# Cross-attention in fp32 from paired fp32r products: the division of the softmax moved from VectorE to ScalarE

## The chip, the cores and the metric

The kernel runs on one core of a Trainium2 chip. The metric is the device time of one execution in microseconds (us). The core has engines with a queue of instructions each: the matrix engine TensorE (PE), VectorE (DVE), ScalarE (ACT), GpSimd (POOL) and SyncE (SP), which here only starts transfers. Each engine takes its own instructions in order; between engines order is kept by semaphores.

## The reference

Input are `x` and `ctx`, each 8 batches of 256 tokens by 512. A first layer mixes them without a softmax. Then the data pass two cross-attention layers of 16 heads of width 128 and an MLP of width 2048, each behind a layer norm and added to its input. Cut to the attention:

```
h = layer_norm(x)
qh, kh, vh = heads(h @ wq + bq), heads(ctx @ wk + bk), heads(ctx @ wv + bv)
kh, vh = concat(kh, bias_k), concat(vh, bias_v)        # one more key and value: 257
logits = einsum('bqhk,bthk->bhqt', qh, kh) / sqrt(128)
weights = softmax(logits, axis=-1)
x = x + einsum('bhqt,bthk->bqhk', weights, vh).reshape(b, q, 2048) @ wo + bo
```

All is float32.

## The kernel before

Every large product is made from three matmuls in the fp32r type (`product`, lines 487 to 491): both operands are held as a high part and a low part, and hi*hi, lo*hi and hi*lo are summed in PSUM. So each result that is to be an operand again is split: ScalarE writes the high part (`qT_hi`, `kT_hi`, `v_hi`, `PT_hi`, `oT_hi`), and VectorE then the rest (`qT_lo` and so on). The weights are split by GpSimd, a cast (line 398) and a subtraction (line 400) of 128x1024 for each matrix.

The batches are done in two halves of four. A half is the first layer, two attention layers and the MLP. An attention layer is eight bodies, one for each pair of heads: FIRST, six MIDDLE in a loop, and LAST (FINAL in the second layer). A body has units of projection (q, k, v and the output product w, 2048 columns wide in two halves or one) in a ring of four PSUM banks `U`, and eight items. An item is one head of one batch: its logits go to `S` (step L), the softmax gives `probs`, PE transposes them to `T` (step T), ScalarE and VectorE split them into `PT_hi` and `PT_lo`, and PE multiplies them with the values into `O` (step P). The order is written out by hand in `ORDER` (lines 105 to 114) as one string for each kind of body, and every engine walks the same string:

```
MIDDLE: "uuuu L0 uuu L1 T0 uu P0 u L2 T1 uu P1 u L3 T2 uu P2 u L4 T3 uu P3 u "
        "L5 T4 uu P4 u L6 T5 uu P5 L7 T6 uu P6 u T7 uu P7 uuu",
```

`u` is half a unit. PE does these steps as written. VectorE takes the row maximum at L (line 1018), and at T the low part of the turned item (line 1032) and then `divide` of the item after it (lines 1020 to 1028). ScalarE at T turns the high part (line 813) and then does `softmax` of the item after (lines 800 to 808): two exponentials of 128x257, each with its sum in `sums`. `divide` waits for them, takes the reciprocal `rs`, waits for that, and multiplies `probs` in place in two instructions of 128x256, after which `a_prob` lets PE transpose. `probs`, `nm`, `sums` and `rs` have two slots each, `S`, `T` and `O` one. In between, ScalarE and VectorE do the splits of the units at their `u` (lines 785 to 798 and 985 to 1008), among them the two small copies that put the extra key into `kT` (line 943).

Of the kernel before, what the change touches and what calls it, by code (L numbers as in the profile page):

```python
# [30 lines left out]
ALU = mybir.AluOpType  # L31
ACT = mybir.ActivationFunctionType
# [35 lines left out]
def units_of(kind):  # L68

    return [u for u in UNITS_A if kind != FINAL or u[0] not in "KV"]  # L70
# [7 lines left out]
def before(half, e, what):  # L78

    return half * ((HBODIES - 1) * per_body(what) + per_body(what, FINAL)) + e * per_body(what)  # L80


def nth(units, c, what):

    return sum(u[0] in what for u in units[:c + 1])
# [31 lines left out]
def steps(kind):  # L117

    halves = [(c, s) for c, u in enumerate(units_of(kind)) for s in ((1,) if u[0] == "w" else (0, 1))]
    normed = int(kind == FIRST)  # L120
    out = []
    for word in ORDER[kind].split():
        if word[0] == "u":
            for _ in word:
                out.append(("U", *halves.pop(0)))
        elif word == "Z":
            out.append(("Z", normed))
        elif word[0] == "A":
            out.append(("A", normed, int(word[1:])))
        else:  # L130
            out.append((word[0], int(word[1:])))
    assert not halves
    return out


def norm_units(kind):

    after = steps(kind)
    after = after[[a[0] for a in after].index("Z"):]
    begun = [a[1] for a in after if a[0] == "U" and (a[2] == 0 or units_of(kind)[a[1]][0] == "w")]  # L140
    assert len({c % RING for c in begun[:CH]}) == CH
    return begun[:CH]


def item(j):

    return j // 4, (j % 4) // 2, j % 2
# [30 lines left out]
def bass_xattn(nc, x_in, ctx_in, thw, thb, pgw, pgb, www, bncol, wa, wk, wv, wb, hcol, vrow,  # L178
               lncol, f1col, orow, out):
    ctx = ExitStack()  # L180
    with ctx:
        def sb(name, shape, dt=F32):
            return ctx.enter_context(nc.sbuf_tensor(name, [P, *shape], dt))
# [5 lines left out]
        def sem(name):  # L189
            return ctx.enter_context(nc.semaphore(name))  # L190
# [32 lines left out]
        probs = sb("probs", [2, 2, 258])  # L223
# [18 lines left out]
        rs = sb("rs", [2, 2])  # L242
# [41 lines left out]
        a_max, a_exp, a_rcp, a_prob = (sem("a_" + s) for s in ("max", "exp", "rcp", "prob"))  # L284
# [6 lines left out]
        def bank(c):  # L291
            return U[:, c % RING, :]

        def qslot(part, h):
            return qT[part][:, h, :]

        def kview(part, p, h):
            return kT[part][:, p, h, :, 0:256]

        def vview(part, p, pair_of):  # L300
            return v[part][:, p, 2 * pair_of:2 * pair_of + 2, :]

        def two(ap):
            return ap.rearrange("p (a n) -> p a n", a=2)

        def kept(eng, value):

            return value if isinstance(value, int) else eng.snap(value)

        def wait_apart(eng, sem, value):  # L310


            eng.wait_ge(sem, value)
            eng.sem_inc(apart, 1)
# [413 lines left out]
        def _(act):  # L728
# [37 lines left out]
            def norm(l, li, p, ch, c):  # L766

                k = CH * p + ch
                wait_apart(act, ln_T, l * TURNS + k + 1)
                wait_apart(act, ln_h, l * TURNS + k - 1 + CR2)  # L770
                act.activation(aff[:, k % 2, :], bank(c), ACT.Identity, bias=lnc[:, 1, li * CH + ch:li * CH + ch + 1],
                               scale=lnc[:, 0, li * CH + ch:li * CH + ch + 1]).then_inc(ln_affine, 1)
                act.wait_ge(ln_affine, l * TURNS + k + 1)
                act.activation(hT[0][:, ch, p * 512:p * 512 + 512], aff[:, k % 2, :], ACT.Copy).then_inc(ln_hi, 1)

            def attention(half, layer, g, kind):
                e = layer * BODIES + g
                n = half * HBODIES + e
                units = units_of(kind)
                ub = act.snap(before(half, e, ALL))  # L780
                jb = act.snap(n * ITEMS)
                vu = act.snap(before(half, e, VS))
                head = kept(act, e * 2)

                def unit_hi(c):

                    what, p, i = units[c]
                    if what == "q":
                        wait_apart(act, a_unit, ub + c + 1 + CR1)
                        act.activation(qslot(0, i), bank(c), ACT.Identity,  # L790
                                       bias=hc[:, 0, bass.ds(head + i, 1)]).then_inc(a_hi, 1)
                    elif what in "kK":
                        wait_apart(act, a_unit, ub + c + 1 + CR1)
                        act.activation(kview(0, p, i), two(bank(c)), ACT.Identity,
                                       bias=hc[:, 1, bass.ds(head + i + 2 * (what == "K"), 1)]).then_inc(a_hi, 1)
                    elif what in "vV":
                        act.wait_ge(a_v32, vu + nth(units, c, VS))
                        act.activation(vview(0, p, i), two(tmp[:, i, :]), ACT.Copy).then_inc(a_hi, 1)  # L798

                def softmax(j):  # L800

                    act.wait_ge(a_max, jb + j + 1)
                    act.wait_ge(a_T, jb + j - 1 + CR2)
                    for qt in range(2):
                        ins = act.activation(probs[:, j % 2, qt, 0:257], S[:, qt, 0:257], ACT.Exp,  # L805
                                             bias=nm[:, j % 2, qt:qt + 1], scale=-1.0,
                                             accum_out=sums[:, j % 2, qt:qt + 1])
                    ins.then_inc(a_exp, 1)

                def turned_hi(j):  # L810
                    act.wait_ge(a_T, jb + j + 1 + CR2)
                    act.wait_ge(a_pv, jb + j + CR1)
                    act.activation(PT[0][:], T[:], ACT.Copy).then_inc(a_pthi, 1)  # L813

                def o_hi(j):
                    p, h, b = item(j)
                    wait_apart(act, a_pv, jb + j + 1 + CR1)
                    act.activation(oT[0][:, p, h, b * 256:b * 256 + 256], O[:, 0:256], ACT.Identity,
                                   bias=hc[:, 3, bass.ds(head + h, 1)]).then_inc(a_ohi, 1)

                for what, *a in steps(kind):
                    if what == "U":
                        if a[1] == 1:
                            unit_hi(a[0])
                    elif what == "L":
                        if a[0] == 0:
                            softmax(0)
                    elif what == "T":
                        turned_hi(*a)
                        if a[0] + 1 < ITEMS:  # L830
                            softmax(a[0] + 1)
                    elif what == "P":
                        o_hi(*a)
                    elif what == "A":
                        nxt = layer if kind == FIRST else layer + 1
                        norm(half * NORMS + nxt, nxt, *a, norm_units(kind)[a[1]])
# [38 lines left out]
        def _(dve):  # L875
# [98 lines left out]
            def attention(half, layer, g, kind):  # L974
# [4 lines left out]
                jb = dve.snap(n * ITEMS)  # L979
# [40 lines left out]
                def divide(j):  # L1020

                    r = j % 2
                    dve.wait_ge(a_exp, jb + j + 1 + CR1)
                    dve.reciprocal(rs[:, r, :], sums[:, r, :]).then_inc(a_rcp, 1)
                    dve.wait_ge(a_rcp, jb + j + 1)
                    for qt in range(2):
                        ins = dve.tensor_scalar(probs[:, r, qt, 0:256], probs[:, r, qt, 0:256], rs[:, r, qt:qt + 1], None, ALU.mult)  # L1027
                    ins.then_inc(a_prob, 1)

                def turned_lo(j):  # L1030
                    dve.wait_ge(a_pthi, jb + j + 1)
# [143 lines left out]
```

## Time and profile before

| | us |
|---|---|
| median of 3 runs | 2548.98 (2546.78 to 2550.6) |
| the profiled execution | 2550.43 |
| its span | 2548.4 |
| PE busy in it | 2422.2 |
| VectorE busy | 1752.9 |
| ScalarE busy | 910.9 |
| GpSimd busy | 668.1 |

The span is the time from the first to the last instruction of the core. An engine that is busy for most of it has little room; the others are idle while they wait, and that costs nothing unless the first waits for them. A mean duration can hide a mixture, so that the smallest, the middle and the largest are read beside it. The mean granted clock of TensorE over the span was 0.984 of full speed.

### The profile page before, as it was taken

Reading aid. Unit: us, or ns where it says so; the run is one execution under the profiler, and the core shown is the slowest. Engines: PE = TensorE matmul, PEld = TensorE weight load, DVE = VectorE, ACT = ScalarE, POOL = GpSimd, SP = SyncE. Lnnn points to the kernel's source line nnn. Section 1 sums busy time; section 2 is a strip of 40 time slices with the busy share of each in tenths; the row PEclk is TensorE's granted clock in tenths of the full one; section 3 lists DMA queues with packets and bytes.
Section 4 is the critical chain, followed back from the end, with each engine's and each line's share of the span. In section 5 each row is a group of like instructions: output and inputs, shape, how many; then the busy total and the mean of one; then the engine's idle time right before and its main releaser. Section 6 shows DMA issues by size and latency. Waiting matters only on the chain.

```text
span 2548.4 us, 41898 instructions
## 1 busy us (share of the span) xinstructions
PE 2422.2 (95%) x13840; PEld 2101.8 (82%) x13840; DVE 1752.9 (69%) x3076; ACT 910.9 (36%) x2142; POOL 668.1 (26%) x427
## 2 busy tenths in 40 slices
PE   7999999999999999889999999999999999997998
PEld 5888888887888888768878888888888888886787
DVE  5777777678776776765567666777876677777555
ACT  3433333344333333411144333334343334333110
POOL 3322222223222222233312222222322222223322
PEclk9999999999999999989999999999999999999999
DMA  3111111111111111111301111111011111110111
GB/s 132 38 38 37 37 37 37 41 38 38 39 37 37 37 37 41 34 33 49 134 34 38 38 37 45 37 37 41 30 38 38 40 42 37 37 41 27 40 49 58
DMA packets 37507, 110.74 MB, mean 43 GB/s; under 512 B 4272, under 2 KB 5168, under 8 KB 37424
## 3 DMA queue, kind: packets, MB, share of 16 engines
q1 hardware_dynamic: 35312, 105.49, 12.3%
q10 hardware_dynamic: 2112, 4.19, 0.4%
q8 instruction: 46, 0.75, 0.1%
q14 instruction: 37, 0.30, 0.0%
HBM read 105.48 MB, written 4.19 MB: 43 GB/s over the span
## 4 chain that ended last, share of the span: by engine, by line
PE 65%; DVE 14%; issue 12%; ACT 6%; POOL 1%; DMA 1%; DVEq 0%; ACTq 0%; SPq 0%; POOLq 0%; PEldq 0%
PE U L489 17%; PE U L491 17%; PE U L490 17%; DVE probs L1027 3%; PE T L646 3%; ACT probs L805 3%; PE S L489 2%; DVE nm L1018 2%; PE S L491 2%; PE S L490 2%; ACT v_hi L798 2%; DVE v_lo L955 2%; DVE tmp L951 2%; DVE z L911 1%; PE O L491 1%
## 5 line engine op out<-in xcount | busy, mean ns | idle before, releaser
L1027 DVE TENSOR_SCALAR probs<-probs,rs 128x256 f32<-128x256 f32 x512 | 375.5, 775 | 9.0
L489 PE MATMUL U<-wos_hi,oT_hi 128*128 128x512 f32 x768 | 311.8, 406 | 11.5 <-DVE oT_lo L1095 6.8
L490 PE MATMUL U<-wos_lo,oT_hi 128*128 128x512 f32 x768 | 305.2, 397 | 0.0
L491 PE MATMUL U<-wos_hi,oT_lo 128*128 128x512 f32 x768 | 305.2, 397 | 0.0
L489 PE MATMUL U<-hT_hi,wqs_hi 128*128 128x512 f32 x768 | 302.7, 394 | 0.0
L490 PE MATMUL U<-hT_lo,wqs_hi 128*128 128x512 f32 x768 | 300.1, 391 | 0.0
L491 PE MATMUL U<-hT_hi,wqs_lo 128*128 128x512 f32 x768 | 299.9, 390 | 0.0
L489 PE MATMUL U<-wvs_hi,cT_hi 128*128 128x256 f32 x1024 | 297.9, 291 | 0.0
L490 PE MATMUL U<-wvs_lo,cT_hi 128*128 128x256 f32 x1024 | 290.0, 283 | 0.0
L805 ACT ACTIVATE probs<-S,nm 128x257 f32<-128x257 f32 x512 | 238.5, 473 | 143.8 <-DVE nm L1018 139.5
L491 PE MATMUL U<-wvs_hi,cT_lo 128*128 128x256 f32 x1024 | 289.9, 283 | 0.0
L398 POOL CAST wos_hi<-raw_ok 128x1024 fp32r<-128x1024 f32 x48 | 50.0, 1042 | 829.7 <-PE U L491 829.7
L813 ACT ACTIVATE PT_hi<-T 128x512 fp32r<-128x512 f32 x256 | 152.6, 596 | 282.4 <-PE T L646 282.4
L1032 DVE TENSOR_TENSOR PT_lo<-T,PT_hi 128x512 fp32r<-128x512 f32 x256 | 175.9, 687 | 51.9 <-ACT PT_hi L813 51.9
L489 PE MATMUL U<-cT_hi,wks_hi 128*128 128x512 f32 x512 | 210.5, 411 | 0.0
L1007 DVE TENSOR_TENSOR x<-x,U 128x512 f32<-128x512 f32 x256 | 169.5, 681 | 49.8 <-PE U L491 49.6
L491 PE MATMUL U<-cT_hi,wks_lo 128*128 128x512 f32 x512 | 201.4, 393 | 0.0
L490 PE MATMUL U<-cT_lo,wks_hi 128*128 128x512 f32 x512 | 200.8, 392 | 0.0
L991 DVE SCALAR_TENSOR_TENSOR qT_lo<-U,hc,qT_hi 128x512 fp32r<-128x512 f32 x128 | 95.7, 747 | 150.0 <-ACT qT_hi L790 150.0
L490 PEld LDWEIGHTS U<-wvs_lo,cT_hi 128*128 128x128 f32 x1024 | 196.0, 191 | 1.3
L489 PEld LDWEIGHTS U<-wvs_hi,cT_hi 128*128 128x128 f32 x1024 | 196.0, 191 | 1.1
L491 PEld LDWEIGHTS U<-wvs_hi,cT_lo 128*128 128x128 f32 x1024 | 195.8, 191 | 0.0
(101 smaller groups left out, 5406.7 us busy)
## 6 DMA issues: line engine op xcount, KB each, us to landing
raw_vq<-wa SPq DMA_DIRECT2D x49, 512.0 KB, 3.3
raw_ok<-wb SPq DMA_DIRECT2D x48, 512.0 KB, 4.5
raw_ok<-wk SPq DMA_DIRECT2D x33, 512.0 KB, 3.3
raw_vq<-wv SPq DMA_DIRECT2D x33, 512.0 KB, 3.3
raw_vb<-vrow SPq DMA_DIRECT2D x33, 256.0 KB, 3.5
c<-ctx_in SPq DMA_DIRECT2D x8, 512.0 KB, 7.6
x<-x_in SPq DMA_DIRECT2D x8, 512.0 KB, 8.5
out<-x ACTq DMA_DIRECT2D x4, 1024.0 KB, 5.4
```

Of the source, the lines that this page charges most:

```text
L489: pe.matmul(o, lhs[0], rhs[0], start=start, stop=False)
L490: pe.matmul(o, lhs[0], rhs[1], start=False, stop=False)
L491: return pe.matmul(o, lhs[1], rhs[0], start=False, stop=stop)
L646: mm = pe.transpose(T[:, tt, qt * P:qt * P + P], probs[:, j % 2, qt, tt * P:tt * P + P], ident[:])
L798: act.activation(vview(0, p, i), two(tmp[:, i, :]), ACT.Copy).then_inc(a_hi, 1)
L805: ins = act.activation(probs[:, j % 2, qt, 0:257], S[:, qt, 0:257], ACT.Exp, bias=nm[:, j % 2, qt:qt + 1], scale=-1.0, accum_out=sums[:, j ...
L813: act.activation(PT[0][:], T[:], ACT.Copy).then_inc(a_pthi, 1)
L951: dve.tensor_tensor(two(tmp[:, i, :]), two(bank(c)), vb[:].unsqueeze(1).to_broadcast([P, 2, 256]), ALU.add).then_inc(v32, 1)
L991: ins = dve.scalar_tensor_tensor(out=qslot(1, i), in0=bank(c), scalar=hc[:, 0, bass.ds(head + i, 1)], in1=f(qslot(0, i)), op0=ALU.add, op1 ...
L1007: ins = dve.tensor_tensor(x[:, t, :], x[:, t, :], bank(c), ALU.add)
L1027: ins = dve.tensor_scalar(probs[:, r, qt, 0:256], probs[:, r, qt, 0:256], rs[:, r, qt:qt + 1], None, ALU.mult)
L1032: dve.tensor_tensor(PT[1][:], T[:], f(PT[0][:]), ALU.subtract).then_inc(a_pt, 1)
```

## The change

The two multiplications leave `divide` on VectorE, which keeps the reciprocal. On ScalarE a new function `divided` follows each `softmax`: it waits for the reciprocal and writes `probs` in place with two Copy activations whose scale is the column `rs`. The semaphores, their counts and the buffers stay.

```diff
@@ -807,6 +807,14 @@
                                              accum_out=sums[:, j % 2, qt:qt + 1])
                     ins.then_inc(a_exp, 1)
 
+                def divided(j):
+
+                    act.wait_ge(a_rcp, jb + j + 1)
+                    for qt in range(2):
+                        ins = act.activation(probs[:, j % 2, qt, 0:256], probs[:, j % 2, qt, 0:256], ACT.Copy,
+                                             scale=rs[:, j % 2, qt:qt + 1])
+                    ins.then_inc(a_prob, 1)
+
                 def turned_hi(j):
                     act.wait_ge(a_T, jb + j + 1 + CR2)
                     act.wait_ge(a_pv, jb + j + CR1)
@@ -825,10 +833,12 @@
                     elif what == "L":
                         if a[0] == 0:
                             softmax(0)
+                            divided(0)
                     elif what == "T":
                         turned_hi(*a)
                         if a[0] + 1 < ITEMS:
                             softmax(a[0] + 1)
+                            divided(a[0] + 1)
                     elif what == "P":
                         o_hi(*a)
                     elif what == "A":
@@ -1022,10 +1032,6 @@
                     r = j % 2
                     dve.wait_ge(a_exp, jb + j + 1 + CR1)
                     dve.reciprocal(rs[:, r, :], sums[:, r, :]).then_inc(a_rcp, 1)
-                    dve.wait_ge(a_rcp, jb + j + 1)
-                    for qt in range(2):
-                        ins = dve.tensor_scalar(probs[:, r, qt, 0:256], probs[:, r, qt, 0:256], rs[:, r, qt:qt + 1], None, ALU.mult)
-                    ins.then_inc(a_prob, 1)
 
                 def turned_lo(j):
                     dve.wait_ge(a_pthi, jb + j + 1)
```

On ScalarE, in the MIDDLE body behind the transposition of item 0 (line numbers from 809 on move with the change). `oT_hi` is the high part of the attention's output. Before:

```order
L813 ACTIVATE PT_hi<-T 128x512
L802 REGISTER_ALU
L805 ACTIVATE probs,sums<-S,nm 128x257 x2
L313 REGISTER_ALU
L794 ISA
L794 ACTIVATE kT_hi<-U,hc 128x2x256
L818 ISA
L818 ACTIVATE oT_hi<-O,hc 128x256
```

Now:

```order
L821 ACTIVATE PT_hi<-T 128x512
L802 REGISTER_ALU
L805 ACTIVATE probs,sums<-S,nm 128x257 x2
L814 ACTIVATE probs<-probs,rs 128x256 x2
L313 REGISTER_ALU
L794 ISA
L794 ACTIVATE kT_hi<-U,hc 128x2x256
L826 ISA
L826 ACTIVATE oT_hi<-O,hc 128x256
```

The pair stands between item 1's exponentials and the high part of `kT`; the rest keeps its order.

On VectorE, at the same place of the MIDDLE body; ISA and REGISTER_ALU are waits and their arithmetic, `bkx` holds the extra key. Before:

```order
L1032 TENSOR_TENSOR PT_lo<-T,PT_hi 128x512
L1023 REGISTER_ALU
L1024 RECIPROCAL rs<-sums 128x2
L1027 TENSOR_SCALAR probs<-probs,rs 128x256 x2
L995 REGISTER_ALU
L943 REGISTER_ALU
L943 COPY kT_hi<-bkx_hi 128x2x2
L943 REGISTER_ALU
L943 COPY kT_lo<-bkx_lo 128x2x2
L945 REGISTER_ALU
L946 ISA
L946 SCALAR_TENSOR_TENSOR kT_lo<-U,hc,kT_hi 128x2x256
```

Now:

```order
L1038 TENSOR_TENSOR PT_lo<-T,PT_hi 128x512
L1033 REGISTER_ALU
L1034 RECIPROCAL rs<-sums 128x2
L1005 REGISTER_ALU
L953 REGISTER_ALU
L953 COPY kT_hi<-bkx_hi 128x2x2
L953 REGISTER_ALU
L953 COPY kT_lo<-bkx_lo 128x2x2
L955 REGISTER_ALU
L956 ISA
L956 SCALAR_TENSOR_TENSOR kT_lo<-U,hc,kT_hi 128x2x256
```

The small copies now follow the reciprocal directly.

## Rows read from the trace of the kernel before

**Rows 1.** The page, its first part: busy us (share of the span) xinstructions.

```profile
PE 2422.2 (95%) x13840; PEld 2101.8 (82%) x13840; DVE 1752.9 (69%) x3076; ACT 910.9 (36%) x2142; POOL 668.1 (26%) x427
```

**Rows 2.** Busy time by stretch, one MIDDLE body: PE, PEld, DVE, ACT, POOL, clock.

```profile
658.30:719.75 61.45, 60.36 (x371) 53.49 (x370) 43.68 (x80) 23.91 (x60) 14.51 (x9) 1.00 0.11 40
```

**Rows 3.** Waits of PE: who waited for whom, us in total, times, longest.

```profile
PE O L489 <- DVE PT_lo L1032: 36.3, 37, 3.0
...
PE S L489 <- DVE qT_lo L991: 13.0, 32, 1.4
```

**Rows 4.** Timeline of PE at gap A: start us, us, engine line.

```profile
667.61 0.28 PE L491 MATMUL U<-wvs_hi,cT_lo 128*128 128x256 f32 x1
668.64 0.39 PE L489 MATMUL O<-PT_hi,v_hi 128*128 128x256 f32 x1 [0.74 <-DVE PT_lo L1032]
668.86 0.28 PE L490 MATMUL O<-PT_lo,v_hi 128*128 128x256 f32 x1
```

**Rows 5.** Timeline of PE at gap B.

```profile
676.63 0.39 PE L491 MATMUL U<-hT_hi,wqs_lo 128*128 128x512 f32 x1
677.36 0.38 PE L489 MATMUL S<-kT_hi,qT_hi 128*128 128x258 f32 x1 [0.34 <-DVE qT_lo L991]
```

**Rows 6.** Timeline of VectorE ahead of gap A.

```profile
660.67 3.53 DVE L1027 TENSOR_SCALAR probs<-probs,rs 128x256 f32<-128x256 f32 x2
...
665.32 0.68 DVE L951 TENSOR_TENSOR tmp<-U,vb 128x512 f32<-128x512 f32 x1
...
667.90 0.68 DVE L1032 TENSOR_TENSOR PT_lo<-T,PT_hi 128x512 fp32r<-128x512 f32 x1
```

**Rows 7.** Timeline of GpSimd at the same time.

```profile
660.53 1.04 POOL L398 CAST wks_hi<-raw_ok 128x1024 fp32r<-128x1024 f32 x1 [9.33 <-PE U L491]
661.66 2.39 POOL L400 TENSOR_TENSOR wks_lo<-raw_ok,wks_hi 128x1024 fp32r<-128x1024 f32 x1
```

**Rows 8.** Timeline of VectorE ahead of gap B.

```profile
674.17 2.40 DVE L1027 TENSOR_SCALAR probs<-probs,rs 128x256 f32<-128x256 f32 x2
676.49 0.74 DVE L991 SCALAR_TENSOR_TENSOR qT_lo<-U,hc,qT_hi 128x512 fp32r<-128x512 f32 x1
```

**Rows 9.** Line 1027: duration ns min/median/max, first and last start us, forms.

```profile
L1027 DVE TENSOR_SCALAR probs<-probs,rs x512: 341/354/2576, 79.7 to 2335.3; 128x256 f32<-128x256 f32 x171
```

**Rows 10.** Groups of instructions: busy us, mean ns, idle before.

```profile
L1027 DVE TENSOR_SCALAR probs<-probs,rs 128x256 f32<-128x256 f32 x512 | 375.5, 775 | 9.0
...
L818 ACT ACTIVATE oT_hi<-O,hc 128x256 fp32r<-128x256 f32 x256 | 120.4, 470 | 210.3 <-PE O L491 209.8
...
L798 ACT ACTIVATE v_hi<-tmp 128x512 fp32r<-128x512 f32 x124 | 78.4, 632 | 233.6 <-DVE tmp L951 233.6
...
L1024 DVE RECIPROCAL rs<-sums 128x2 f32<-128x2 f32 x256 | 42.5, 166 | 119.3 <-ACT probs L805 119.3
```

**Rows 11.** Timeline of ScalarE at items 1 and 3 of this body.

```profile
659.87 0.48 ACT L805 ACTIVATE probs<-S,nm 128x257 f32<-128x257 f32 x1
660.22 0.21 ACT L805 ACTIVATION_READ_ACCUMULATOR probs<-S,nm 128x1 f32 x1
...
673.83 0.69 ACT L790 ACTIVATE qT_hi<-U,hc 128x512 fp32r<-128x512 f32 x1
```

**Rows 12.** Timeline of VectorE in the FIRST body of layer 1.

```profile
595.96 1.01 DVE L943 CAST kT_hi<-bkx_hi 128x4 fp32r<-128x4 f32 x1
596.88 0.16 DVE L943 CAST kT_lo<-bkx_lo 128x4 fp32r<-128x4 f32 x1
```

**Rows 13.** Timeline of PE: a LAST body, then the FINAL body of the first half.

```profile
546.07 0.47 PE L489 MATMUL U<-wos_hi,oT_hi 128*128 128x512 f32 x1 [0.49 <-DVE oT_lo L1038]
...
1045.98 0.38 PE L489 MATMUL S<-kT_hi,qT_hi 128*128 128x258 f32 x1 [1.44 <-DVE qT_lo L991]
...
1052.77 0.66 PE L646 MATMUL T<-ident,probs 128*128 128x128 f32 x4 [1.12 <-DVE probs L1027]
...
1062.46 0.58 PE L489 MATMUL O<-PT_hi,v_hi 128*128 128x256 f32 x1 [2.33 <-DVE PT_lo L1032]
```

## The prediction, made before the changed kernel ran

> **What bounds the kernel now.** I read the page's first part, then the busy time by stretch, the waits of the matrix engine (PE), and last the timeline around those waits. PE is busy for 95% of the span, VectorE for 69%, ScalarE for 36% [rows 1]; the end is set by PE's queue, and a change elsewhere counts only where PE waits. An attention layer is 8 bodies: one FIRST, six MIDDLE, one LAST (in layer 1 FINAL). A MIDDLE body lasts 61.45 us with PE busy for 60.36 at the full granted clock, 1.00 [rows 2]. By groups, PE waits 36.3 us in 37 places for `PT_lo` and 13.0 us in 32 for `qT_lo`, both made by VectorE [rows 3].
>
> Two places in a MIDDLE body hold them. Before item 1's value product (`O`), the matmul of 667.61 should be followed 0.12 us later, as 256-column ones are, at 667.73; the next starts at 668.64 and its successor 0.22 later in place of 0.12: 0.91 + 0.10 = 1.01 us lost [rows 4]. This is gap A. Before item 4's logits (`S`), 512-column matmuls follow each other by 0.23, so 676.86 was due and 677.36 came: 0.50, with the same slow second one 0.60 [rows 5]. This is gap B. Together 1.6 us a body.
>
> **What makes them.** Gap A ends with `PT_lo` of 667.90, behind `v_lo`, behind `v_hi`, behind `tmp` at 665.32, behind `kT_lo`, and that behind item 1's two multiplications, which took 3.53 us from 660.67 [rows 6]. GpSimd's cast runs from 660.53 to 661.57 and its subtraction from 661.66 to 664.05 [rows 7]; each multiplication ends just after one of them. Gap B ends with `qT_lo` at 676.49, behind item 3's pair of 2.40 us from 674.17 [rows 8]. Line 1027 takes 341 ns at least, 354 in the middle, 2576 at most [rows 9] and 775 in the mean [rows 10]: 512 x (775 - 354) = 216 us of it is being held up. The stall and not the work makes the gaps.
>
> **The change part by part.**
> *Removed:* 512 multiplications, 375 us of VectorE [rows 10]. Nearly all of it lies beside PE's work; on the path to the end are only the gaps, so it is worth these and no more.
> *Added on ScalarE:* 512 copies of 128x256, SBUF to SBUF, scaled by a column. No row has this form. From below: the 128x512 SBUF copy without a column takes 632 ns, and half of it would be 316; from above 632 itself; nearest is 128x256 from PSUM with a column operand, 470 [rows 10]. I take 0.50 (470 and a little for SBUF) and, since ScalarE's instructions overlap by some 0.1 (an exponential of 0.48 from 659.87 is followed at 660.22 [rows 11]), 0.91 a pair; bounds 0.6 and 1.3.
> *Added wait:* ScalarE stands until the reciprocal is there: 0.17 [rows 10] and some 0.08 around it. The reciprocal stays where it is, and in front of it stands `PT_lo` of the item before, which begins with the exponentials at the latest and takes 0.69, less than the two exponentials' 1.0. So 0.25 + 0.91 = 1.16 us more of ScalarE's queue per item, 297 us over 256 items, on an engine that is idle 64% of the time. Queued behind it are `kT_hi`, `qT_hi`, `v_hi` or a norm's `aff`, and VectorE waits for those.
>
> *Gap A replayed.* The exponentials' sums are read by 660.43 [rows 11]; the pair then runs 660.70 to 661.61, `kT_hi` to 662.3, `kT_lo` on VectorE to 663.0. Counted back from 667.73, 30 matmuls at 0.12 and four transposes, some 4.0, the unit of `v` that `tmp` reads has its last matmul issued at 663.6 and ended by 663.9, so `tmp` begins at 664.0 in place of 665.32: 1.3 us earlier, and with it `v_hi`, `v_lo`, the maximum and `PT_lo`, ready at 667.3 (+0.05), when PE wants it at 667.73. Slack 0.4, gap A gone.
> *Gap B replayed* (clock of before). `qT_hi` now begins at 673.83 behind item 3's exponentials [rows 11]; with 1.16 before it, it begins at 675.0 and ends at 675.7; `qT_lo`, 0.75 long, to 676.5, and PE wants it at 676.86. But with gap A gone VectorE is 1.2 to 1.7 us ahead at item 3 and PE only 1.0, which leaves the slack at 0.5 to 1.0. Gap B gone; it would return with a pair of over 1.4. `v_lo`'s earlier end lets GpSimd start its next split, and the load behind that, 1.7 us sooner against VectorE; nothing that GpSimd can hold is in VectorE's queue there any more.
> Nothing else in the body is close: PE takes the probabilities a whole item (4.6 us or more) after the logits, and the new path from maximum to probabilities is 0.75 + 0.95 + 0.25 + 0.91 = 2.9.
>
> **The sum.**
> MIDDLE: 24 x 1.6 = 38.4.
> LAST: gaps A and B, 0.49 idle and 0.16 of slow start before the output product at 546.07, which item 4's held pair delays through `oT_lo` [rows 13], and about 0.6, an unheld pair, out of VectorE's queue in front of the layer norm: 2.9 x 2 = 5.8.
> FINAL: idle of 1.44 before `S` at 1045.98, 1.12 before `T` at 1052.77 and 2.33 before `O` at 1062.46 [rows 13]. The first two come from held pairs and go nearly whole; the third falls with VectorE's queue but keeps 1.5, since transposition, `PT_hi` and `PT_lo` follow each other with nothing between. With A (1.01) 1.0 + 1.3 + 1.1 + 0.8 and 1.0 from the work on `x` and its statistics that now comes earlier: 5.2 x 2 = 10.4.
> FIRST: only B, 0.6 x 4 = 2.4; its other gaps hang on the norm's work, which GpSimd holds up still.
> MLP and the first layer: nothing.
> Sum 57.0. Against the profiled execution's 2550.43 us (span 2548.4 and 2.0 around it) that is 2493.4; this execution lies 1.5 above the median of the runs. I say 2493.
>
> **Rules of the skill.** In sentences that the sum can do without: the Trainium skill (ScalarE: Activation LUTs, Rules for kernel authors) says to give multiplications to VectorE and not to ScalarE, as it is faster per element. The trace agrees on the bare instruction (354 ns against my 500) and not on the mean (775). By the rule alone the change would cost about 0.3 us a pair on a chain through it and 1.2 on ScalarE's queue, which is rival 4. The Trainium skill (SBUF — State Buffer, its part on the shared port pair) says that whichever of a two-port VectorE operation and a GpSimd operation starts first holds the pair and the other waits. That names what rows 6 and 7 show, and makes rival 1.
>
> **The rivals.**
> 1. *The stall moves to the next instruction.* Freed of the multiplications, VectorE comes at 660.70 to the two small copies into `kT`, within GpSimd's cast. If the second falls behind the subtraction, it is held until 664.05, as the pair was, and gap A stays in 28 bodies: 28 x 1.0, so 2521. For it: these copies are of the kind that can be held; in a FIRST body one took 1.01 us from 595.96. Against: there the second took 0.16 from 596.88 and slipped in between [rows 12]; the same order of events is due here.
> 2. *ScalarE's instruction is held as VectorE's was*, or is dear for another reason. A pair of 2 to 3 us at items 1, 3 and 4 brings B back, 24 x 0.6 = 14, or with most of A 24 x 1.4 = 34, and up to 10 in FINAL: 2507 to 2537. Against: no ScalarE row in [rows 10] spreads like line 1027.
> 3. *No change:* the gaps are set by the chain of `v_hi` and `tmp` and come back whole elsewhere: 2549. Against it: rows 6 to 8 tie both gaps to the held pairs.
> 4. *Slower:* ScalarE's queue sets the joints of the layers. The norm's eight groups (`aff`, `hT_hi`) stand behind a softmax; if each starts 1.2 us later and PE waits for it, that is 8 x 1.2 = 9.6, and where the gaps stay as in 3 the time is 2559. It decides once the pair and wait delay `aff` past the transposes' end; in most of the eight ScalarE waits there for VectorE or PE now, which speaks against it.
> That the change doesn't do what it says is hardly a rival: the order of ScalarE's instructions shows the pairs, and no table load more.
>
> **How the numbers follow.** My forecast has 0.66, own range 2484 to 2505 (pair at 0.6 or 1.3, FINAL 2 us either way each, LAST and FIRST halved). Rival 1 has 0.13, rival 2 0.10, no change 0.05, slower 0.06. The range 2484 to 2530 holds nearly all of the first two and half of rival 2. A measurement of this kernel can tell 0.2%, 5 us: faster by more 0.89, within 0.05, slower 0.06.
>
> **What would show it.** Right: MIDDLE bodies of 59.9 us, no wait of PE for `PT_lo` or `qT_lo` in them; pairs on ScalarE of 0.9, the same at all eight items; VectorE at 1380 us, ScalarE at some 1150; the small copies at item 1 held for 1 us at most. Wrong: a copy of 2.3 us there and gap A as before (rival 1), pairs that spread (rival 2), `aff` late with PE waiting (rival 4). The weakest step is the slack of 0.4 and 0.5 us at the gaps: a pair over 1.4, or a reciprocal that comes late, takes B back first.

## The result, and the profile after

The changed kernel takes 2483.35 us (median of 4 runs, 2479.96 to 2486.31), against 2548.14 for the kernel before in the same runs: a ratio of 0.9744 [0.9727, 0.9761]. The forecast was 2493 with a range from 2484 to 2530. It is faster in the way forecast, by more than forecast, and the time lies 0.65 us below the range. The profiled execution took 2486.31, the slowest of the four, with a span of 2484.5, which is 63.9 less than before.

The page's first part, answering to [rows 1] (busy us, share of the span, instructions):

```profile
PE 2396.6 (96%) x13840; PEld 2095.1 (84%) x13840; DVE 1419.6 (57%) x2564; ACT 1131.5 (46%) x2654; POOL 666.6 (27%) x427
```

VectorE is 333 us less busy, ScalarE 221 us more, and PE 26 us less for the same 13840 matmuls. One MIDDLE body, answering to [rows 2] (columns as there):

```profile
641.60:701.43 59.83, 59.83 (x371) 53.52 (x369) 32.91 (x65) 30.82 (x76) 14.46 (x9) 1.00 0.11 41
```

PE is busy for all of it: the body is now as long as its matmuls. The waits of PE, answering to [rows 3] (who waited for whom, us in total, times, longest):

```profile
PE U L581 <- DVE z L921: 25.0, 6, 5.9
PE O L489 <- DVE PT_lo L1038: 14.1, 10, 2.4
PE S L489 <- ACT probs L805: 12.4, 4, 3.5
...
PE T L646 <- ACT probs L814: 0.8, 2, 0.6
```

Of 37 waits for `PT_lo` 10 are left, none of them in a MIDDLE body, and the row for `qT_lo` is gone. What remains stands at the layers' joints. PE at the places of gap A and gap B, answering to [rows 4, 5]:

```profile
650.76 0.28 PE L491 MATMUL U<-wvs_hi,cT_lo 128*128 128x256 f32 x1
650.88 0.28 PE L489 MATMUL O<-PT_hi,v_hi 128*128 128x256 f32 x1
...
658.77 0.39 PE L491 MATMUL U<-hT_hi,wqs_lo 128*128 128x512 f32 x1
659.00 0.28 PE L489 MATMUL S<-kT_hi,qT_hi 128*128 128x258 f32 x1
```

The matmuls follow each other by 0.12 and 0.23, as inside a run of them. VectorE (its last row is ahead of B) and then GpSimd, answering to [rows 6 to 8]:

```profile
644.29 0.46 DVE L953 CAST kT_hi<-bkx_hi 128x4 fp32r x1
644.66 0.16 DVE L953 CAST kT_lo<-bkx_lo 128x4 fp32r x1
645.93 0.75 DVE L956 SCALAR_TENSOR_TENSOR kT_lo<-U,hc,kT_hi 128x512 fp32r<-128x512 f32 x1 [1.11 <-ACT kT_hi L794]
...
647.05 0.69 DVE L961 TENSOR_TENSOR tmp<-U,vb 128x512 f32<-128x512 f32 x1
...
649.65 0.68 DVE L1038 TENSOR_TENSOR PT_lo<-T,PT_hi 128x512 fp32r<-128x512 f32 x1
...
657.61 0.75 DVE L1001 SCALAR_TENSOR_TENSOR qT_lo<-U,hc,qT_hi 128x512 fp32r<-128x512 f32 x1 [1.55 <-ACT qT_hi L790]
```

```profile
643.69 1.04 POOL L398 CAST wks_hi<-raw_ok 128x1024 fp32r<-128x1024 f32 x1 [9.34 <-PE U L491]
644.81 2.41 POOL L400 TENSOR_TENSOR wks_lo<-raw_ok,wks_hi 128x1024 fp32r<-128x1024 f32 x1
```

The first small copy ends 0.02 after GpSimd's cast; the second begins 0.15 before the subtraction and costs 0.16. While the subtraction runs, from 644.81 to 647.22, where a pair of multiplications used to be held, VectorE first waits for `kT_hi` until 645.93 and then starts three instructions, `kT_lo`, `oT_lo` and `tmp`, which each read one operand from PSUM and take their usual 0.75, 0.47 and 0.69 us. `PT_lo` is ready at 650.33, 0.55 before PE takes it, and `qT_lo` at 658.36, 0.64 before. ScalarE at items 1 and 3, answering to [rows 11]:

```profile
644.30 0.91 ACT L814 ACTIVATE probs<-probs,rs 128x256 f32<-128x256 f32 x2 [0.23 <-DVE rs L1034]
645.12 0.67 ACT L794 ACTIVATE kT_hi<-U,hc 128x512 fp32r<-128x512 f32 x1
...
656.09 0.91 ACT L814 ACTIVATE probs<-probs,rs 128x256 f32<-128x256 f32 x2 [0.23 <-DVE rs L1034]
656.91 0.67 ACT L790 ACTIVATE qT_hi<-U,hc 128x512 fp32r<-128x512 f32 x1
```

And all 512 copies by duration, answering to [rows 9] (ns, min/median/max):

```profile
L814 ACT ACTIVATE probs<-probs,rs x512: 492/502/512, 79.4 to 2272.3; 128x256 f32<-128x256 f32 x171
```

Line 1027 spread from 341 to 2576 ns; these spread from 492 to 512. The bare instruction has become 42% dearer and the whole kernel 2.6% faster.

**Where the 63.9 us came from.** I cut both spans at the first transposition of each body's item 0, and let the last part run to the end of the span; another 0.2 lies before the first cut:

| part | before | after | gained | forecast |
|---|---|---|---|---|
| 24 MIDDLE bodies | 1474.5 | 1435.2 | 39.3 | 38.4 |
| 2 LAST | 149.7 | 142.9 | 6.9 | 5.8 |
| 2 FINAL, with all that follows up to the next half or the end | 577.9 | 564.5 | 13.4 | 10.4 |
| 4 FIRST | 265.3 | 261.2 | 4.1 | 2.4 |

### The profile page after: what moved, and what is told of

It is laid out like the page before. It is cut to its first block, busy times and chain, and to the rows that moved or that the text cites. A ratio compares the mean times of both kernels' runs of the same rounds, so it can differ in the third digit from the quotient of the medians.

```text
span 2484.5 us, 41898 instructions
## 1 busy us (share of the span) xinstructions
PE 2396.6 (96%) x13840; PEld 2095.1 (84%) x13840; DVE 1419.6 (57%) x2564; ACT 1131.5 (46%) x2654; POOL 666.6 (27%) x427
## 4 chain that ended last, share of the span: by engine, by line
PE 85%; issue 7%; DVE 3%; POOL 2%; ACT 2%; DMA 1%; ACTq 0%; SPq 0%; POOLq 0%; DVEq 0%; PEldq 0%
PE U L489 22%; PE U L491 22%; PE U L490 22%; PE T L646 4%; PE S L491 2%; PE S L489 2%; PE O L489 2%; PE S L490 2%; PE O L491 2%; PE O L490 2%; DVE z L921 1%; PE U L547 1%; DMA raw_vq<-wa 1%; PE U L551 0%; POOL x L423 0%
## 5 line engine op out<-in xcount | busy, mean ns | idle before, releaser
L814 ACT ACTIVATE probs<-probs,rs 128x256 f32<-128x256 f32 x512 | 233.0, 502 | 59.5 <-DVE rs L1034 59.5
L790 ACT ACTIVATE qT_hi<-U,hc 128x512 fp32r<-128x512 f32 x128 | 87.6, 684 | 294.4 <-PE U L491 294.4
L1028 DVE TENSOR_REDUCE nm<-S 128x2 f32<-128x514 f32 x256 | 175.9, 687 | 39.5 <-PE S L491 39.4
```

What stands on the lines that cost most here:

```text
L790: act.activation(qslot(0, i), bank(c), ACT.Identity, bias=hc[:, 0, bass.ds(head + i, 1)]).then_inc(a_hi, 1)
L814: ins = act.activation(probs[:, j % 2, qt, 0:256], probs[:, j % 2, qt, 0:256], ACT.Copy, scale=rs[:, j % 2, qt:qt + 1])
L1028: dve.tensor_reduce(nm[:, j % 2, :], S[:, :, 0:257], AX.X, ALU.min).then_inc(a_max, 1)
```

## The experiments

Theory 1 (held instructions): gaps A and B exist because GpSimd holds VectorE's multiplications at items 1 and 3, and for no other reason. Theory 2 (less work): VectorE gained by having less to do, wherever the work was. The last five runs ask why the sum was too small, and what is left. `z` written in the fifth and sixth experiment is free space in a MIDDLE body; nobody reads what is put there.

**1. Only items 1 and 3 divided on ScalarE**, the other six on VectorE as before:

```diff
@@ divided, ScalarE
+if not (j in (1, 3)):
+    return
 act.wait_ge(a_rcp, jb + j + 1)
...
@@ divide, VectorE
 dve.reciprocal(rs[:, r, :], sums[:, r, :]).then_inc(a_rcp, 1)
+if j in (1, 3):
+    return
+dve.wait_ge(a_rcp, jb + j + 1)
+for qt in range(2):
+    ins = dve.tensor_scalar(probs[:, r, qt, 0:256], probs[:, r, qt, 0:256], rs[:, r, qt:qt + 1], None, ALU.mult)
+ins.then_inc(a_prob, 1)
```

> Theory 1 (held pairs): the gain comes from taking away a VectorE instruction that GpSimd's splits hold, and only at items 1 and 3 does PE wait for it in a MIDDLE body. With the division of items 1 and 3 alone on ScalarE a MIDDLE body lasts 59.8 us as with all eight moved, and the whole is 2495 to 2505 us, since item 4's held pair stays in FINAL. Theory 2 (less work): the gain of 65 us comes from 0.6 us less work per item on VectorE; two items of eight give a quarter of it, 2532 us.

Measured: 2491.13 us, 0.9778 [0.9761, 0.9796], and MIDDLE bodies of 59.77 to 59.83. A quarter of the instructions moved and the MIDDLE bodies gained all that they can. To the changed kernel 8 us are missing between the medians and 5.4 between the two profiled executions; of these 3.4 lie in the two LAST (73.2 each, not 71.4) and 1.5 in FINAL. Theory 2 falls. The time is still 4 us better than the lower end expected.

**2. The complement**: items 0, 2, 5, 6, 7 on ScalarE; 1, 3 and 4 stay on VectorE (the condition above is `j not in (1, 3, 4)`).

> Items 0, 2, 5, 6 and 7 alone are divided on ScalarE, 1, 3 and 4 stay on VectorE. Theory 1 (held pairs): nothing held is removed, MIDDLE bodies stay at 61.4 to 61.5 us, the whole within 5 us of 2548. Theory 2 (less work): five eighths of the gain, 2508 us.

Measured: 2534.18, 0.995 [0.9931, 0.9968]; MIDDLE 60.9 to 61.0. Neither theory said this. Gap A stands whole (PE):

```profile
664.82 0.39 PE L489 MATMUL O<-PT_hi,v_hi 128*128 128x256 f32 x1 [0.74 <-DVE PT_lo L1046]
```

Gap B is nearly gone, although item 3's pair is held (VectorE, then GpSimd):

```profile
670.13 2.17 DVE L1041 TENSOR_SCALAR probs<-probs,rs 128x256 f32<-128x256 f32 x2
```

```profile
667.88 1.04 POOL L398 CAST wvs_hi<-raw_vq 128x1024 fp32r<-128x1024 f32 x1 [7.64 <-DVE v_lo L967]
669.00 2.41 POOL L400 TENSOR_TENSOR wvs_lo<-raw_vq,wvs_hi 128x1024 fp32r<-128x1024 f32 x1
```

GpSimd's cast begins at the end of `v_lo`, and here its subtraction starts 1.13 us ahead of the pair; in the kernel before it was 0.90 (673.27 against 674.17 of [rows 8]). So the pair is held 0.23 less, 2.17 for 2.40. Counted from the start of the body (658.29 in the kernel before, 654.47 here) it also starts 0.23 earlier, so that it ends 0.45 earlier, and that is the whole of the 0.46 that B lost. Both halves come from item 2's pair, which no longer stands ahead of `tmp`: `v_lo` ends 0.46 earlier, and the subtraction starts at 14.53 in place of 14.98. Theory 1 in its strict form, one held pair for each gap and nothing else, holds for A and fails for B: how much of a hold an instruction catches depends on where GpSimd's work begins, which VectorE's own `v_lo` sets.

**3. All on VectorE, in a form with one operand in PSUM**: the kernel before, with the multiplication issued as scalar_tensor_tensor, whose second tensor (`T`) is bypassed.

```diff
+dve.memset(T[:], 1.0).then_inc(ones_in, 1)     # once, at the start
+dve.wait_ge(ones_in, 1)
...
-ins = dve.tensor_scalar(probs[:, r, qt, 0:256], probs[:, r, qt, 0:256], rs[:, r, qt:qt + 1], None, ALU.mult)
+ins = dve.scalar_tensor_tensor(out=probs[:, r, qt, 0:256], in0=probs[:, r, qt, 0:256], scalar=rs[:, r, qt:qt + 1],
+                               in1=T[:, qt, :], op0=ALU.mult, op1=ALU.bypass)
```

> All divisions stay on VectorE, but as scalar_tensor_tensor with a second operand in PUSM that is bypassed, a form that with a PSUM operand was never held in the trace (0.47 us each, in place of 0.35 unheld). Theory 1 (held pairs): no instruction is held, MIDDLE bodies 59.8 us, the whole 2480 to 2495. Theory 2 (less work): VectorE has 0.25 us more of work per item than before, so 2548 or more.

Measured: 2486.93, 0.9769 [0.975, 0.9787], with MIDDLE bodies of 59.76 to 59.83. Its line:

```profile
L1030 DVE SCALAR_TENSOR_TENSOR probs<-probs,rs,T x512: 473/479/483, 79.4 to 2273.4; 128x256 f32<-128x256 f32 x171
```

Never under 473 ns and never over 483, where the form before had 341 to 2576. This is the sharpest run for theory 1: VectorE keeps all the work, each instruction is 35% dearer than an unheld one, and the time is that of the changed kernel within 4 us. The Trainium skill (SBUF — State Buffer, Who interferes with whom) says that a VectorE instruction with at most one input in SBUF, outside its two-port modes, doesn't contend with GpSimd. The row agrees. It says also that ScalarE has ports of its own; the 492 to 512 ns of the copies agree with that.

**4. The hold made shorter**: the kernel before, with GpSimd's subtraction of 128x1024 cut into four.

```diff
-return pool.tensor_tensor(hi_lo[1][:], raw, f(hi_lo[0][:]), ALU.subtract)
+lo, hi = hi_lo[1][:], f(hi_lo[0][:])
+for i in range(4):
+    if raw.shape[1] == 4:
+        at = (slice(None), i, slice(None))
+    else:
+        at = (slice(None), i // 2, slice(i % 2 * 256, i % 2 * 256 + 256))
+    ins = pool.tensor_tensor(lo[at], raw[at], hi[at], ALU.subtract)
+return ins
```

> The kernel before, with GpSimd's subtraction of 128x1024 cut into four of 128x256 (some 0.8 us each by line 405). Theory 1 (held pairs): a multiplication is held by at most 1.1 us; gap B goes and most of gap A, MIDDLE bodies 60.0 to 60.8, the whole 2500 to 2530. Theory 2 (less work): VectorE's work is the same, 2548.

Measured: 2479.57, 0.9738 [0.9716, 0.976], as fast as the changed kernel without moving anything. The division in it:

```profile
L1034 DVE TENSOR_SCALAR probs<-probs,rs 128x256 f32<-128x256 f32 x512 | 261.6, 552 | 9.0
```

And GpSimd's four pieces:

```profile
661.03 2.88 POOL L406 TENSOR_TENSOR wqs_lo<-raw_vq,wqs_hi 128x256 fp32r<-128x256 f32 x4
```

They take 2.88 us in place of 2.4 [rows 7], and the mean of the held instruction falls from 775 ns [rows 10] to 552. MIDDLE bodies are at 59.76 to 59.83: what is left of the hold fits into the slack. I had expected 2500 to 2530.

**5. The hold alone put back**: the changed kernel, and on VectorE behind each reciprocal of a MIDDLE body two tensor_scalar of 128x256, the same form at the same place as before.

```diff
 dve.reciprocal(rs[:, r, :], sums[:, r, :]).then_inc(a_rcp, 1)
+if kind == MIDDLE:
+    dve.wait_ge(a_rcp, jb + j + 1)
+    dve.wait_ge(spare, spent + j + CR1)
+    for qt in range(2):
+        ins = dve.tensor_scalar(z[:, qt, 0:256], z[:, 2 + qt, 0:256], rs[:, r, qt:qt + 1], None, ALU.mult)
+    ins.then_inc(spare, 1)
```

> The changed kernel, and in the 24 MIDDLE bodies VectorE does two more tensor_scalar of 128x256 from SBUF to SBUF after each reciprocal, on data that nobody reads. The division stays on ScalarE. Theory 1 (held pairs): the pair is held as before at items 1, 3 and 4, gaps A and B come back without the probabilities being late: MIDDLE bodies 61.2 to 61.6 us, the whole 2518 to 2526. Rival (the gain came from ScalarE's earlier probabilities): MIDDLE stays at 59.8, 2483.

Measured: 2527.6, 0.9926 [0.9909, 0.9942], 1.6 us above what theory 1 had; MIDDLE 61.45 to 61.77, so all 40 us of it are given back. PE's waits:

```profile
PE O L490 <- DVE PT_lo L1046: 32.0, 34, 2.4
...
PE S L490 <- DVE qT_lo L1003: 10.3, 24, 0.4
```

24 waits more for each of the two than in the changed kernel, one a body. The held pairs behind them (VectorE, items 1 and 3; between them item 2's, not held):

```profile
654.03 2.76 DVE L1041 TENSOR_SCALAR z<-z,rs 128x256 f32<-128x256 f32 x2 [0.48 <-DVE rs L1036]
...
661.95 0.61 DVE L1041 TENSOR_SCALAR z<-z,rs 128x256 f32<-128x256 f32 x2
...
666.93 2.32 DVE L1041 TENSOR_SCALAR z<-z,rs 128x256 f32<-128x256 f32 x2
```

**6. A second pair of scaled copies on ScalarE** in MIDDLE bodies, behind the first: the slack that I had put at 0.4 to 1.0 us is asked for directly.

```diff
 ins.then_inc(a_prob, 1)
+if kind == MIDDLE:
+    act.wait_ge(spare, spent + j + CR1)
+    for qt in range(2):
+        ins = act.activation(z[:, qt, 0:256], z[:, 2 + qt, 0:256], ACT.Copy, scale=rs[:, j % 2, qt:qt + 1])
+    ins.then_inc(spare, 1)
```

> The changed kernel, and in the 24 MIDDLE bodies ScalarE does a second pair of scaled copies behind the first, on data that nobody reads: 1.8 us for the pairs and 2.05 with the reciprocal's wait. The forecast said that gap B comes back with over 1.4 for the pair by the clock of before, and put 0.5 to 1.0 us of slack at B and 0.4 at A. If that holds, B returns by up to 0.5 and A by up to 0.6: 60.2 to 60.9 us a body, 2493 to 2509. If ScalarE's queue has more room than I gave it, MIDDLE stays at 59.8 and the whole at 2483 to 2486.

Measured: 2530.71, 0.9941 [0.9924, 0.9958]; 1.8 us more in every MIDDLE body, and 22 us above the most that I had expected. B was expected to return, since `qT_hi` waits for 0.9 more; A came back too, at 0.84. VectorE, GpSimd and ScalarE ahead of A:

```profile
655.45 0.17 DVE L960 CAST kT_hi<-bkx_hi 128x4 fp32r x1
655.56 2.36 DVE L960 CAST kT_lo<-bkx_lo 128x4 fp32r x1
```

```profile
654.34 1.04 POOL L399 CAST wks_hi<-raw_ok 128x1024 fp32r<-128x1024 f32 x1 [9.34 <-PE U L492]
655.46 2.43 POOL L401 TENSOR_TENSOR wks_lo<-raw_ok,wks_hi 128x1024 fp32r<-128x1024 f32 x1
```

```profile
657.08 0.67 ACT L796 ACTIVATE kT_hi<-U,hc 128x512 fp32r<-128x512 f32 x1
```

A copy of four columns is held for 2.36 us, and so in all 24 MIDDLE bodies. That is my rival 1, happening: here the first copy came behind the cast, so the second fell behind the subtraction, while in the changed kernel the first was caught by the cast and the second slipped between. But it isn't what brought A back. The next instruction, `kT_lo`, needs `kT_hi`, which ScalarE ends at 657.75, and starts 0.14 behind it at 657.89, as it starts 0.14 behind `kT_hi` in the changed kernel (645.79 and 645.93); it is 0.14 in all 24 bodies. Counted from the body's start `kT_hi` ends 1.31 us later than there: 0.79 from the second pair at item 1, and 0.52 because the second pair at item 0 delays that item's `kT_hi`, the next maximum and with it item 1's exponentials. Against a slack of 0.55 that is gap A, by ScalarE's queue alone. The expectation had counted the second pair once on the way to A, and it stands there twice. In the changed kernel, where `kT_hi` is ready long before the subtraction ends at 647.22, a held copy would have put `kT_lo` off from 645.93 by 1.3 us (an estimate), more than the slack: that it slipped through, by 0.15 us, was luck in the order of two engines.

**7. Only the FINAL bodies divided on ScalarE** (`kind == FINAL` as the condition), to see whether that term was mis-sized in itself.

> Only the two FINAL bodies divide on ScalarE. The sum gave 5.2 us each, the changed kernel showed 6.4 and 7.1 from the FINAL body to the next half or the end. If the missing part is the granted clock after shorter waits, this kernel shows less time at the lower clock behind FINAL and gains 12 to 14 us, 2534 to 2536. If it came from the other bodies, it gains 10, 2538.

Measured: 2533.57, 0.9943 [0.9924, 0.9963], 0.4 us below the expected range; 13.5 us between the medians and 15.3 off the span, with the MIDDLE bodies as before (1473.9 in all) and all the gain in the two FINAL parts (8.2 and 7.4). The changed kernel, with the same FINAL, gained 6.4 and 7.0 there. The granted clock answers for part of it, as the next section works out: TensorE spent 83 us at the lower of its two levels (1.2 GHz) in the kernel before, 68 here, 61 in the changed kernel. Two stretches of 30 us of the first FINAL, that of before and that of the changed kernel, with about the same work. Columns as in [rows 2]: behind the five engines stands the clock, 0.83 and then 0.94:

```profile
1060.00:1090.00 30.00, 22.02 (x98) 18.29 (x96) 21.21 (x45) 12.22 (x24) 8.41 (x7) 0.83 0.00 1
```

```profile
1028.00:1058.00 30.00, 20.49 (x104) 16.62 (x103) 21.08 (x42) 14.71 (x29) 9.35 (x8) 0.94 0.00 1
```

**8. The changed kernel with GpSimd's bias addition held off `z`**: it waits until all four tiles of a group are normalised, and so cannot hold VectorE between them.

```diff
-pool.wait_ge(ln_z, l * TILES + t + 1)
+pool.wait_ge(ln_z, l * TILES + 4 * p + 4)
```

> The changed kernel, and GpSimd adds the output bias to x only when all four tiles of the norm are done, so that it doesn't hold them: z took 1.48 us a tile against 0.54 unheld. PE waits 25.0 us for z in six places and for what stands behind z in more. Theory 1 applied to GpSimd's additions: z's four tiles take 2.2 to 3.5 us in place of 5.6 to 6.6, so 2 to 4 us at each of six norms, 12 to 24 in all, less what the later additions hold of the split of hT: 2460 to 2472. If z is not held but slow of itself: 2483 or more.

Measured: 2465.29, 0.9685 [0.9669, 0.9701], 18 us below the changed kernel. The norm's line, in the changed kernel and then here:

```profile
L921 DVE TENSOR_SCALAR z<-x,mv,rstd 128x512 f32<-128x512 f32 x48 | 62.0, 1353 | 4.1 <-POOL rstd L416 4.1
```

```profile
L921 DVE TENSOR_SCALAR z<-x,mv,rstd 128x512 f32<-128x512 f32 x48 | 39.0, 875 | 4.1 <-POOL rstd L416 4.1
```

The middle duration of the line falls from 1482 to 543 ns; its longest, 2.62 us, stays, so some tiles are still held. PE's wait for `z` falls from 25.0 to 13.6 us. The same mechanism was at work in the joints, at a line that the change didn't touch; the prediction had said of FIRST that its gaps hang there.

**9. The changed kernel with the four pieces**, to see whether experiment 4 and the change pay twice.

> The changed kernel with GpSimd's subtraction in four pieces. The kernel before with pieces (e4) measured 2479.6. Theory 1 (held pairs): with short holds it matters little where the division is done, so that this one lies within 6 us of e4, 2474 to 2485. If moving the division brought a gain of its own beside the holds, it would show here as 10 us or more below e4.

Measured: 2465.84 (5 runs), 0.9685 [0.9672, 0.9698], 14 us below experiment 4, whose MIDDLE bodies are the same, so all of it at the joints. I had expected 6 at most if only the holds count, and named 10 or more as the sign of a gain of its own: so moving the division has one, outside the MIDDLE bodies. Between the two spans (2478.3 and 2463.5) PE is busy for 9.1 us less with the same matmuls (2394.3 and 2385.2) and idle for 5.7 less; the time at the lower clock falls from 56 to 33 us.

**10. The kernel before with late bias and pieces**, and **11. the changed kernel with both.**

> The kernel before with GpSimd's subtraction in pieces and its bias additions after all four tiles of the norm. The two take away holds at different places and should add: 2479.6 - 18 = 2462, in 2455 to 2470. If the multiplications of VectorE are held by the additions now, more than 2470.

> The changed kernel with both. By the sum of the single effects 2465.3 (late additions) less 0 to 8 for the pieces, 2457 to 2466. It should be the fastest of all if ScalarE's longer queue doesn't matter at the joints of the layers, and slower than the kernel before with both where it does.

Measured: 2469.72 (5 runs), 0.9701 [0.9688, 0.9715], and 2453.28 (5 runs, 2452.39 to 2455.12), 0.9633 [0.962, 0.9646]: the fastest version here, 30 us below the changed kernel. The effects don't add: the late additions and the pieces bring 18 and 17.5 us alone on the changed kernel and 30 together (4 below what I expected), and on the kernel before the pieces leave 10 us to the additions, where I had 18. Once both cures for GpSimd's holds are in, moving the division still brings 16 us, none of it in MIDDLE bodies (1435.4 and 1435.2). Half of it is PE's busy time (2393.3 and 2385.6); time at the lower clock: 48 and 31 us. PE's two chief waits on VectorE in experiment 11:

```profile
PE U L588 <- DVE z L928: 12.0, 4, 3.3
...
PE O L496 <- DVE PT_lo L1045: 5.5, 7, 1.7
```

## Why the prediction was right in its mechanism and short in its sum

**The two gaps** (right). Forecast 1.01 + 0.60 a MIDDLE body; the starts of the matmuls show 1.00 to 1.02 at A and 0.60 at B, and the bodies 39.3 in 24, against 38.4. That the stall and not the work makes them is shown from four sides: moving two items of eight is enough (1), the same work in a form that GpSimd can't hold is enough (3), a shorter hold is enough (4), and the hold on data nobody needs brings both gaps back (5). The slack forecast at A was 0.4 and at B 0.5 to 1.0; it is 0.55 and 0.64.

**The copies** (right, but for VectorE's busy time). 0.50 and a pair of 0.91 were taken, 502 ns and 0.91 came; the wait for the reciprocal is 0.23, not 0.25. The small copies at item 1 took 0.46 and 0.16 (forecast: 1 us at most). ScalarE came to 1131.5 (some 1150). VectorE came to 1419.6 and not 1380: 15 us are the first small copy, now held by the cast (its mean went from 177 to 296 ns), and the other 25 are overlap that was lost. Instructions that follow each other at once overlap in the records by some 0.1 us, and now more of them stand alone: the overlaps of VectorE come to 129 us before and 82 after, and only 21 of that lay within the pairs that left.

**The step that failed is the sum at the joints.** Where the sum had 57.0, the spans show 63.9: FINAL 13.4 for 10.4, FIRST 4.1 for 2.4, LAST 6.9 for 5.8, MIDDLE 0.9 more. The other 3 of the 10 us between 2493.4 and 2483.35 are the spread of the executions: the profiled one of the changed kernel lies 3.0 above its median. The forecast was also counted from the profiled 2550.43 and not from the median; from 2548.14 the same sum gives 2491.

FINAL, up to the norm: 5.9, not 5.2, in both halves, the same to 0.01 in experiment 7. By the starts of the same matmuls, counted from the body's start, PE gains 1.0 at A with its slow second one, 0.24 around item 2's `O`, 1.37 before `S`, 1.28 before `T`, 0.62 before an output product and 0.62 before the late `O`, 5.16 by then. My own four terms of 1.0, 1.3, 1.1 and 0.8 are right, the two others were missing. The larger one is a wait for `oT_lo` of the kind that the sum has in LAST. PE, before:

```profile
1055.22 0.47 PE L489 MATMUL U<-wos_hi,oT_hi 128*128 128x512 f32 x1 [0.40 <-DVE oT_lo L1038]
...
1063.05 0.41 PE L491 MATMUL O<-PT_hi,v_lo 128*128 128x256 f32 x1
1063.26 0.41 PE L489 MATMUL O<-PT_hi,v_hi 128*128 128x256 f32 x1
...
1070.08 0.47 PE L581 MATMUL U<-ident,z 128*128 128x128 f32 x1 [3.99 <-DVE z L911]
```

And after:

```profile
1030.63 0.39 PE L489 MATMUL O<-PT_hi,v_hi 128*128 128x256 f32 x1 [1.71 <-DVE PT_lo L1038]
...
1031.43 0.28 PE L489 MATMUL S<-kT_hi,qT_hi 128*128 128x258 f32 x1
1031.55 0.28 PE L490 MATMUL S<-kT_lo,qT_hi 128*128 128x258 f32 x1
...
1037.50 3.34 PE L581 MATMUL U<-ident,z 128*128 128x128 f32 x16 [4.62 <-DVE z L921]
```

Before, behind idle times of 1.44, 1.12 and 2.33 us [rows 13], the granted clock was at the lower level and these matmuls were 0.21 apart; after, behind the one of 1.71, they are 0.12 apart. The `O`, `S` and `T` of this place are shorter by 0.64, 0.49 and 0.24 us in themselves. Yet that brings nothing here: PE then waits for `z`, 4.62 in place of 3.99. The way to `z` runs over VectorE alone, from `PT_lo` (1061.72 before, 1029.89 after) over the statistics to `z` (1066.15 and 1033.57), and is 0.75 shorter because a pair has left it; the sum had 1.0 for that.

FINAL, behind the norm: 0.5 and 1.1 more in the changed kernel, 2.3 and 1.5 in experiment 7, where the sum had nothing. This is mostly the clock, a term that the prediction doesn't have. From `z` to the end of the first part the two kernels do the same but for one division, and in the whole part both spend 15.9 us at the lower level. But PE is busy during 13.6 of these in the changed kernel and during 10.4 in experiment 7; half of the difference, 1.6, is about what separates 6.4 from 8.2. In the kernel before it is busy during 19.5 of 24.5, 3.4 of that at the late `O`. So time at the lower level cost half of PE's busy time in it, and nothing where PE waited right behind.

So the 22 us less at the lower level over the whole span (83 to 61) are not 11 us gained. PE's busy time gives a nearer bound: it fell by 25.6 us, 12.7 of that in the MIDDLE bodies, where the clock is at its full level and it belongs to the two gaps with their slow second matmul, and 12.9 at the joints, out of a gain there of 24.6. The level also differs from one execution to the next: the kernel before has taken 2548.67 us at a mean granted clock of 0.984 and 2548.76 at 0.988, which is some 20 us of difference at the lower level and none in time.

FIRST: 4.1, not 2.4, and 3.5 of it in the first one, whose gap I had put down to the norm. In it the held pair pushed the small copies into the subtraction, and PE waited 3.16 us for the `kT_lo` behind them, 1.21 in the changed kernel (VectorE, before):

```profile
83.79 1.45 DVE L1027 TENSOR_SCALAR probs<-probs,rs 128x256 f32<-128x256 f32 x2
...
85.23 2.32 DVE L943 CAST kT_lo<-bkx_lo 128x4 fp32r<-128x4 f32 x1
```

The copy of 2.32 us is rival 1 at work in the kernel before, which the prediction overlooked when it showed only the FIRST body where the copy slipped through; in the changed one no copy of `kT_lo` takes over 173 ns. The other 1.5 us are B and matmuls at the lower clock behind the long wait, less a new wait of 0.74 for `PT_lo`. In the other three FIRST bodies B's 0.6 came, but 0.3 to 0.6 of it was given back. LAST: 6.9, not 5.8: 0.8 and 0.6 before the output product (forecast 0.65 each), then 0.6 at the late `O` and 0.5 behind it, where the sum had 0.6 for the two together.

**The rivals.** Rival 1 did not come with the change but lies 0.15 us beside it: experiment 6 produced the held copy, hidden there behind a later `kT_hi`, so that no run shows its price in a MIDDLE body. Rival 2 is refuted by 492 to 512 ns. Rival 3 is refuted by experiments 1 and 3. Rival 4 (slower at the joints by ScalarE's queue) did not come: at no joint does the changed kernel come later than the kernel before. In the FIRST body of layer 1 PE is up to 1.2 us late at the norm's transpositions, counted from the body's start, but nothing waits there. The matmuls themselves are slower, with a granted clock of 0.53 over the first 5 us of the body against 0.78 before.

**The range** took FINAL's error as 2 us either way each, which gives 2489; no term of the prediction gives the other 5 us down to 2484. Counted from the median, and with the clock's term and a gain at the first FIRST body, it would have begun lower. What stays open: how much of the 12.9 us less of busy PE at the joints is the clock and how much belongs to the waits that went, and why the lower level falls where it does. No run fixed the clock.

## What to carry to other kernels

Where one line's durations spread from 341 through a median of 354 to 2576 ns, the instruction is held and not slow: look on the neighbouring engine for what runs just then, and either give the work to an engine that isn't held, write it in a form that isn't (one operand in PSUM), or cut the holder into pieces; all three brought the same 2.3 to 2.6% here. Then ask which instruction falls into the hold next, since a copy of four columns paid 2.36 us there. And where PE idles for a microsecond or two in a row of short steps, count the matmuls behind as slower too, and give a forecast a term for it; it is worth something only as far as PE doesn't wait again right behind, and it came to 0.5 to 2.3 us for the same stretch of work here. Last, count a forecast from the median of the executions and not from the one that was profiled.

## What the runs showed of the hardware that I had not expected

- A GpSimd subtraction of 128x1024, 2.4 us, holds a VectorE copy of 128x4 as long as it would hold a large one: 2.36 us in place of 0.17.
- scalar_tensor_tensor on VectorE with a bypassed tensor in PSUM costs 479 ns for 128x256 and never varied by over 10 ns, beside a tensor_scalar of 354 ns that varied up to 2576.
- Four subtractions of 128x256 take 2.88 us and one of 128x1024 takes 2.4: 0.5 us more work on GpSimd brought 2.6%.
- The time at TensorE's lower clock went from 83 us (before) to 61 (after) and 31 (fastest) with the same matmuls. Equal times at the lower level are not equal costs: 15.9 us in the first FINAL part of two kernels held 13.6 and 10.4 us of busy PE, and the parts differ by 1.8 us.
